# One cross-attention and expert layer on one core: earlier weight pieces, keys projected once, scores by two row tiles

## What is computed

```python
x = x + xattn(layernorm(x), ctx, ctx, abundance, ...)   # 16 heads of 16, 64 keys
x = x + ffn(layernorm(x), gate_w, expert_bias, w1, w2, w3)  # top 2 of 8 experts
scores = einsum('bhqd,bhkd->bhqk', q, k) * scale + log(abundance)
attn   = softmax(scores)
h = silu(xe @ w1[e]) * (xe @ w3[e]);  out += h @ w2[e]
```

## Time and profile before

| | |
|---|---|
| time, median of 3 runs (lowest to highest) | 461.13 us (460.94 to 462.37) |
| the profiled execution's own time | 461.81 us |
| its span, first to last instruction | 460.1 us |
| busy: PE, DVE, ACT, POOL | 368.7, 258.0, 195.2, 232.2 us |
| share of the chain of waits on PE, DVE, DMA | 70%, 11%, 5% |
| steps before the loop / loop / steps after it / routing / experts | 0 to 78 / 78 to 139 / 139 to 184 / 184 to 218 / 218 to 437 us |

### The profile page before, as it was taken

The page is one execution under the profiler, slowest core; times in us unless marked ns, Lnnn a source line. Parts: engine busy times, 40 slices in busy tenths (PEclk is TensorE's granted clock), DMA queues, the critical chain, the costliest instruction groups (busy, mean ns, idle before and its releaser), DMA issues.

```text
span 460.1 us, 10326 instructions
## 1 busy us (share of the span) xinstructions
PE 368.7 (80%) x2657; PEld 271.7 (59%) x2658; DVE 258.0 (56%) x635; ACT 195.2 (42%) x351; POOL 232.2 (50%) x281
## 2 busy tenths in 40 slices
PE   2765998999999774011899999999999999999830
PEld 1533777777877663010567677767777776777620
DVE  2775666767666216984455555555555555556400
ACT  2155686757576444400334343333443344333300
POOL 6367547443445535803235555655565556565340
PEclk9865999999999665555999999999999999999985
DMA  5904253323336262302367777777777777788636
GB/s 152 351 23 139 59 206 110 119 77 125 108 120 195 73 213 68 103 0 49 79 131 131 133 134 132 132 136 138 138 139 135 136 134 136 133 135 133 98 56 194
DMA packets 106677, 57.55 MB, mean 125 GB/s; under 512 B 82581, under 2 KB 101282, under 8 KB 106626
## 3 DMA queue, kind: packets, MB, share of 16 engines
q1 hardware_dynamic: 98848, 46.78, 40.4%
q0 software_dynamic: 7488, 10.39, 15.4%
q10 hardware_dynamic: 322, 0.15, 0.1%
HBM read 28.62 MB, written 11.60 MB: 87 GB/s over the span
## 4 chain that ended last, share of the span: by engine, by line
PE 70%; DVE 11%; DMA 5%; issue 5%; POOL 3%; ACT 2%; POOLq 0%; SPq 0%; DVEq 0%; ACTq 0%
PE sc L1353 11%; PE sc L1355 10%; PE sc L1354 10%; PE bank L1238 5%; PE bank L1369 5%; PE bank L1372 5%; PE bank L1371 4%; PE bank L1307 3%; PE ptps L1283 3%; POOL w_lo L526 2%; DMA acc<-xn,put_now 2%; PE bank L1296 2%; DMA w_hi<-n_L_xattn_in_proj_weight 1%; PE sc L1162 1%; DVE arena L850 1%
## 5 line engine op out<-in xcount | busy, mean ns | idle before, releaser
L1353 PE MATMUL sc<-w_hi,arena 128*128 x312 | 98.5, 316 | 12.2 <-DMA arena<-xn 8.9
L1354 PE MATMUL sc<-w_hi,arena 128*128 x312 | 98.1, 315 | 0.0
L1355 PE MATMUL sc<-w_lo,arena 128*128 x312 | 98.1, 314 | 0.0
L609 POOL DMA_INDIRECT acc<-xn,put_now x39 | 62.5, 1601 | 70.5 <-DVE xn L1121 58.5
L526 POOL TENSOR_TENSOR w_lo<-stage_w,w_hi 128x1408 f16<-128x1408 f32 (+3 forms) x32 | 71.8, 2256 | 45.7 <-ACT w_hi L633 45.0
L1108 DVE SCALAR_TENSOR_TENSOR arena<-sc,slot_score,arena 128x352 f32<-128x352 f32 x78 | 45.5, 584 | 85.1 <-ACT arena L778 83.8
L778 ACT ACTIVATE arena<-sc,slot_score 128x352 f32<-128x352 f32 x78 | 43.1, 553 | 116.9 <-PE sc L1355 116.9
L1369 PE MATMUL bank<-w_hi,arena 128*128 x234 | 63.8, 273 | 3.3 <-DVE xn L1121 1.8
L1372 PE MATMUL bank<-w_lo,arena 128*128 x234 | 61.7, 273 | 0.0
L578 POOL DMA_INDIRECT arena<-table,get_now x39 | 42.4, 1086 | 33.3 <-POOL get_now L575 31.4
L1371 PE MATMUL bank<-w_hi,arena 128*128 x195 | 53.2, 273 | 0.0
(11 more groups left out here) (191 smaller groups left out, 638.3 us busy)
## 6 DMA issues: line engine op xcount, KB each, us to landing
stage_w<-in_L_ffn_w SPq DMA_DIRECT2D x16, 704.0 KB, 4.2
stage_w<-in_L_ffn_w SPq DMA_DIRECT2D x16, 256.0 KB, 2.9
stage_w<-in_L_ffn_w SPq DMA_DIRECT2D x32, 64.0 KB, 2.7
acc<-arena SPq DMA_DIRECT2D x16, 128.0 KB, 1.7
table<-xn SPq DMA_DIRECT2D x16, 128.0 KB, 1.8
arena<-in_x SPq DMA_DIRECT2D x2, 896.0 KB, 6.3
arena<-table,get_now POOLq DMA_INDIRECT x39
arena<-xn SPq DMA_TRANSPOSE x39
```

Source lines behind the costliest of these rows:

```text
L609: pool.indirect_dma_start(out=acc[:, :], out_offset=bass.IndirectOffsetOnAxis(ap=put_now[par][:, 0:1], axis=0), in_=y_sb[par], in_offset=N ...
L1353: pe.matmul(ps[:, c, :], gT[par][:, k, :], w_hi[:, cols], start=k == 0, stop=False)
L1354: pe.matmul(ps[:, c, :], gT[par][:, KD + k, :], w_hi[:, cols], start=False, stop=False)
L1355: ins = pe.matmul(ps[:, c, :], gT[par][:, k, :], w_lo[:, cols], start=False, stop=k == KD - 1)
```

## The change

1. SP loads pieces 0 and 1 before the rest of x (two DMAs of 896 KB), and pieces 2 and 3 after it.
2. ACT casts piece 0 after `tokens_high(0)` and piece 1 after the high half of the query weights; before, both stood behind the copies of the values. POOL makes their low halves ahead of `beta`.
3. An exp of one column is put behind the logarithm at ACT's start.
4. The keys are projected once (128 columns instead of 256); DVE's L836 reads them twice.
5. The block pattern of the keys is by 4 heads instead of 8, so it has 256 columns instead of 512 and half the work in `spread_keys`. Scores are made by `scores`: two bias matmuls of 512 columns first, then 12 matmuls of 256 columns, each over 64 of the 128 rows, the lower and the upper rows in turn, into two banks. The heads come out in another order, which the AV matmuls undo by their index `jv`.
6. PE's list has the whole scores behind AV and the two transposes. DVE's list has both maxima behind `tokens_low`; at steps 0 and 1 the statistics of the first layer norm and the output bias stand behind `queries_low` instead of ahead of the maxima's end.

```diff
@@ SP
             sp.wait_ge(s["wkv_load"], 16)
-            for b in range(B):
+            def load_rest_of_x(b):
                 sp.dma_start(xs[:, b + 2:T:2, :], x[b, P:N, :].rearrange("(u p) d -> p u d", p=P))\
...
-            for n in range(AHEAD):
+            for n in range(2):
+                load(n)
+            for b in range(B):
+                load_rest_of_x(b)
+            for n in range(2, AHEAD):
                 load(n)
@@ POOL
+            for n in range(2):
+                piece_low(n)
+
             pool.wait_ge(s["bias_parts"], 1)
...
             pool.wait_ge(s["kb_dve"], 8)
-            for n in range(AHEAD):
+            for n in range(2, AHEAD):
                 piece_low(n)
@@ ACT
             act.activation(ab_log[:, :], ab_log[:, :], ACT.Ln).then_inc(s["ab_log_s"], 1)
+            act.activation(oT[:, 0:1], ident[:, 0:1], ACT.Exp)
...
             tokens_high(0)
+            piece_high(0)
             act.wait_ge(s["wqT_ps"], 1)
...
                 .then_inc(s["wq_hi_s"], 1)
+            piece_high(1)
             act.wait_ge(s["wvT_ps"], 1)
...
-            piece_high(0)
-            piece_high(1)
-
@@ DVE
+            link(dve.tensor_tensor(half_mask[:, :], head_mask[:, 0:4], head_mask[:, 4:8], ALU.add))
...
-                        dve.tensor_tensor(dst[:, c, b, :].rearrange("p (h s) -> p h s", h=8),
-                                          src[:, c, b:b + 1, :].broadcast_to([P, 8, S2]),
-                                          head_mask[:, :, None].broadcast_to([P, 8, S2]), ALU.mult).then_inc(s["kb_dve"], 1)
+                        dve.tensor_tensor(dst[:, c, b, :].rearrange("p (h s) -> p h s", h=4),
+                                          src[:, c, b:b + 1, :].broadcast_to([P, 4, S2]),
+                                          half_mask[:, :, None].broadcast_to([P, 4, S2]), ALU.mult).then_inc(s["kb_dve"], 1)
...
-                    dve.wait_ge(s["s_ps"], 2 * tt + c + 1)
+                    dve.wait_ge(s["s_ps"], tt + 1)
@@ PE
-            def scores_half(par, c):
...
+            def scores(par):
+
+                for c in range(2):
+                    pe.matmul(sc_ps[par][:, c * HS:(c + 1) * HS], ones16[:, :], beta[:, par, c * HS:(c + 1) * HS],
+                              start=True, stop=False, skip_group_check=True)
+                for c in range(2):
+                    for q, kb, last in ((qT_hi, kb_hi, False), (qT_hi, kb_lo, False), (qT_lo, kb_hi, True)):
+                        for g in range(2):
+                            rows = slice(g * P // 2, (g + 1) * P // 2)
+                            at = g * HS + c * HQ
+                            ins = pe.matmul(sc_ps[par][:, at:at + HQ], q[par][rows, c * P:(c + 1) * P],
+                                            kb[rows, c, par, :], start=False, stop=last, skip_group_check=True)
+                return ins
...
-                    ins = pe.matmul(sc_ps[1][:, c * 512:c * 512 + B * P], wkT[:, k, c * P:(c + 1) * P],
-                                    ctxD[:, k].rearrange("p b r s -> p (b r s)"), start=k == 0, stop=k == KD - 1)
+                    ins = pe.matmul(sc_ps[1][:, c * 512:c * 512 + B * S2], wkT[:, k, c * P:(c + 1) * P],
+                                    ctxD[:, k, :, 0, :], start=k == 0, stop=k == KD - 1)
```

More of the change, by code:

```diff
@@ L85, in xattn_moe @@
         xs = take(T * D).rearrange("p (t d) -> p t d", t=T)
-        kb_hi, kb_lo = (take(2 * B * HS, F16).rearrange("p (c b n) -> p c b n", c=2, b=B) for _ in range(2))
+        HQ = HS // 2
+        kb_hi, kb_lo = (take(2 * B * HQ, F16).rearrange("p (c b n) -> p c b n", c=2, b=B) for _ in range(2))
         wq_hi, wq_lo = (take(KD * D, F16).rearrange("p (k n) -> p k n", k=KD) for _ in range(2))
@@ L190, in xattn_moe @@
         head_mask = take(8)
+        half_mask = take(4)
         zero_rows = take(D)
@@ L514, in _ @@
             assert n_c[0] == N_CONST
-            pool.wait_ge(s["bias_parts"], 1)
-            for b in range(B):
-                pool.tensor_tensor(beta[:, b, :].rearrange("p (h s) -> p h s", h=H),
-                                   bias16[:, b * H:(b + 1) * H, None].broadcast_to([P, H, S2]),
-                                   key_diag[:, None, :].broadcast_to([P, H, S2]), ALU.mult).then_inc(s["beta_s"], 1)
             def weights_low(number, staged, cols):
@@ L953, in step @@
                     beaten(0, EARLY)
-                if here(t, 0):
-                    if t is None or t >= 1:
-                        dve.wait_ge(s["ssub"], tt)
-                    maxima(0)
                 if here(t, 2):
```

76 lines of the change are left out of this document (39 added, 37 removed).

## The result

The changed kernel takes 457.55 us (median of 12 runs, 453.99 to 462.00) beside 461.53 us of the kernel before on the same chips (median of 12); the ratio is 0.990, with a 95% interval of 0.987 to 0.993. One run of the changed kernel, the 462.00, was in a slower state and is left out of the ratio; the other eleven have a median of 456.80. So it is faster, by about 1%, where the forecast of 449.0 was 2.6% faster, and the time lies above the forecast's range. The profiled execution of the changed kernel is one of its faster ones, 455.71 us with a span of 454.0, 6.1 less than the span before.

What follows compares the result with a forecast made beforehand. It took PE as full in the loop, after an early ACT stall; 9.1 (start) + 0.6 (steps 3 to 5) + 2.4 (loop) + 0 = 12.1 us less, from a median of 461.13 to 449.0, range 445.5 to 454.5.

Steps and rivals of the forecast that it cites:

- (a): Start: keys projected once and a shorter `spread_keys(0)` bring the queries of tile 0 from 18.64 to 16.2.
- (b): Start: PE ends its gapless stretch at 23.8, two casts go, and step 0's tokens are served at 27.2, not 31.4.
- (c): Start: ACT's 4.11 us wait for piece 4 goes; scores of step 1 start at 31.0, 7.5 us earlier.
- Beta's cover: Start: beta, behind POOL's two low halves, is ready at 21.5 and PE wants it at 24, 2.5 us spare.
- (d): Steps 1 to 3: statistics leave the way to AV of step 2, 3.1 us earlier, mostly given back at low clock.
- Steps 3 to 5: Stretch behind the start: 0.3 in step 3 and 0.3 for steps 4 and 5, 0.6 us together.
- The loop: Eight steps: shorter scores, then the layer-norm chain bounds; a pair goes from 15.14 to 14.55, 2.4 us less.
- so ACT starts at 3.63: Loop: ACT applies the layer norm's scale and shift 3.63 us behind L1308, with POOL's shift ending at 3.59.
- rivals 1 and 3: Loop: row tiles take turns, 451.0, chance 0.15; every step: full/half-row changes hold PE, 465, chance 0.04.
- The tail: Steps 14 to 19: PE's 3.06 us wait in step 15 for ACT's layer norm stays, gain 0.
- Rival 2: Start: pieces 0 and 1 land 2 to 4 us late; 451 to 453, or 455 with low clock; chance 0.13.
- the fourth: Start: pieces come no earlier, as `beta` or the casts hold the scores; 460 to 462, chance 0.02.

Runs made afterwards that it cites:

- pool_late: The changed kernel with POOL making the low halves of pieces 0 and 1 behind the two beta products instead of ahead; 453.44 us, ratio 0.980.
- scores_only: The changed kernel without the changes of the start (loads, casts, low halves, keys' projection as before); 456.39 us, ratio 0.987.
- warm: The changed kernel with eight extra unread matmuls in step 5, where PE waits for a layer norm; 453.90 us, ratio 0.984.
- defer_only: The changed kernel with POOL's second pieces of steps 4, 14 and 15 put behind the next step's layer norm; 446.73 us, ratio 0.969.
- unrolled: The changed kernel with the loop of the attention steps written out; 447.80 us, ratio 0.969.
- after: The changed kernel itself, compared with the kernel before; 457.55 us, ratio 0.990.
- after_again: The changed kernel once more, unchanged, for a second trace; 455.79 us, ratio 0.987 to the kernel before.

## Why the prediction was wrong

- **(a), the start: the right sum (8.7 beside 9.1) by luck, out of wrong terms.** "`spread_keys(0)` ... 1.2 less" was 2.8 more, because the change also moved POOL's low halves beside it, and I asked of them only whether beta had cover; in other executions the same loss stands in the cast or the product ahead of it. pool_late shows 1.42 without POOL beside. The second `spread_keys` of the trace of before, 5.18 beside `beta`, could have told me. The queries of tile 0 came at 19.85, not 16.2. The casts did cost nothing, and piece 0 was cast by 13.43.
- **(b), (c).** The wait for piece 4 went as forecast, and the scores of step 1 came 5.7 earlier, not 7.5: the tokens of step 0 were served at 29.1 instead of 27.2 (by my own numbers, 24.9 and two casts of 2.1 together, 27.0), for the lateness of (a). That lateness of 3.65 had shrunk to 1.9 by then, as PE went from the queries to the scores of step 0 in 6.32 instead of 7.54 us: part of the values ran at the full clock in this execution and not in the one before. Beta's cover held: it was done ahead of 26.17.
- **(d).** The way from the scores of step 1 to AV of step 2 fell from 9.6 to 5.7, more than the 3.1 I took, which made good part of what (a) had lost; of 9.7 at AV of step 2, 1.0 was given back to step 3, as feared: 8.7 beside 9.1. That scores_only has 4.7 there without the start shows the size of this part.
- **Steps 3 to 5.** "0.6 together" was 1.1 to AV of step 5. But with "none of which changes" I took it that the wait of step 5, whose cause stands in the earlier trace rows, stayed as it was, although PE's own work ahead of it got shorter; it grew from 1.27 to 1.77, the clock fell behind it, and 3.6 went back. This is the first step that failed. warm and defer_only both show it. Whether the half microsecond by which the wait grew made the clock fall isn't shown, since the same wait left it full in unrolled.
- **The loop: the step that failed is "so ACT starts at 3.63".** POOL's end was 3.58 behind the bias product in the odd step, as forecast (3.59), and 3.70 in the even one, and the way from ACT's start to the next product as well (2.51 and 1.97 beside 2.50 and 2.01). But ACT started at 4.00 and 3.85: in the earlier trace rows the work ahead of it accounted for the lateness, and once that was gone I allowed 0.04, which holds for written-out steps only; in the loop the register instructions behind the wait take 0.27 to 0.30. In the loop of before ACT never waited there, so its rows could not show this. The gain of 2.4 was 0.1. PE's side was right or better: the pairs of row tiles run side by side, the scores fell by 0.44 a step, and a switch between full and half rows costs about 0.1 (the two products with `beta` take 0.53 instead of 0.43), so rivals 1 and 3 fall.
- **The tail** changed by 0.2, as good as the forecast's 0. That it held a wait of 3 us of the same cause as step 5's was seen and left at 0; it is still there, 2.82.
- **Rivals.** None was right. The time lies between the 455 of the second and the 460 of the fourth. The fourth's reason is wrong: pieces came earlier, and the gain was lost later. Rival 2 named a stretch that was late, but not the cause; the pieces landed on time.

## What to carry to other kernels

When a change takes work from the engine that bounds a loop, write down the next chain link by link, with the register instructions that stand between a wait and the work behind it; an order of the instruction list shows them, a timeline of busy time does not. When an operation is moved, ask what it now runs beside: products of two SBUF operands on VectorE took four to five times as long beside GpSimd's work here (1.42 us alone, 5.32 and 7.81). And a short wait of TensorE may cost more than its length, if the clock falls behind it (here 1.77 us of wait and 3.6 of clock); take the wait away rather than price it.

## What was not expected of the hardware

- Four products of 128x256 on VectorE took 1.42 us alone and 5.32 or 7.81 beside GpSimd's products; a cast of 128x32 took 2.30 instead of 0.18, and one of 128x256 took 2.91 instead of 0.29. The Trainium skill, SBUF — State Buffer, section "SBUF: two separate sides", says that VectorE and GpSimd share a pair of ports, which one of them holds for a whole instruction while the other is blocked; on VectorE's side it counts instructions with two SBUF inputs and those in a mode that uses both ports. The products' rows agree. A cast has one input; whether these ran in such a mode no run here shows. Operations that read PSUM beside one SBUF operand kept their 0.42 (L873, L867).
- Register instructions behind a wait cost ScalarE 0.27 to 0.30 us of every loop step; 0.14 to 0.21 with the wait moved, 0.04 in the written-out code.
- Twelve half-row matmuls took 0.76 us listed in pairs and 1.00 listed six and six, less than the 1.3 of twelve slots: by the starts, some on one half of the rows began ahead of others that are listed before them.
- The clock fell behind PE's wait of 1.77 us in step 5 in four traces (after, after_again, scores_only, pool_late), and not behind the same wait in unrolled, with the same instructions ahead of it. What decides that stays open.
